# Softmax division of a windowed attention with channels on partitions: reciprocals spread on GpSimd and mapped by one matrix product

## What is computed

```python
x = x + attention(layernorm(x))         # softmax(q k^T / sqrt(8)) v, window 64, then @ Wo.T
x = x + experts(layernorm(x))           # sigmoid gate, 4 of 16 experts, silu(g) * u, plus a shared expert
# in attention:
p = jax.nn.softmax(scores, axis=-1)
out = jnp.einsum('bhnqk,bhnkd->bhnqd', p, v2)
out = out.transpose(0, 2, 1, 3).reshape(B, T, C)
return out @ Wo.T
```

## Time and profile before

| | |
|---|---|
| median of 3 runs | 708.99 us (707.56 to 709.00) |
| profiled execution | 710.96 us, its span 709.2 us |
| busy: PE, PEld, DVE, ACT, POOL | 93%, 74%, 83%, 75%, 67% |
| one slot of the loop | 40.1 us |

### The profile page before, as it was taken

The page is one execution under the profiler, slowest core; times in us unless marked ns, Lnnn a source line. Parts: engine busy times, 40 slices in busy tenths (PEclk is TensorE's granted clock), DMA queues, the critical chain, the costliest instruction groups (busy, mean ns, idle before and its releaser), DMA issues.

```text
span 709.2 us, 20018 instructions
## 1 busy us (share of the span) xinstructions
PE 662.5 (93%) x6488; PEld 521.9 (74%) x6488; DVE 590.6 (83%) x1708; ACT 530.9 (75%) x1635; POOL 478.5 (67%) x599
## 2 busy tenths in 40 slices
PE   3988889999999999999999999999999999989996
PEld 2767657777787877778787877778787877767775
DVE  2777797989989898988989898998989898888663
ACT  3775869787887879787887879787887879763432
POOL 3503157878788787877778687877878686776523
PEclk9998899999999999999999999999999999999999
DMA  6000022040414123040413113040313213041321
GB/s 174 20 13 31 1 73 96 17 141 28 130 50 120 59 74 105 19 131 30 122 58 116 63 63 117 12 137 30 120 59 105 74 56 110 6 134 35 117 76 46
DMA packets 50245, 52.60 MB, mean 74 GB/s; under 512 B 5664, under 2 KB 31904, under 8 KB 50080
## 3 DMA queue, kind: packets, MB, share of 16 engines
q1 hardware_dynamic: 50208, 52.14, 23.7%
HBM read 43.20 MB, written 4.72 MB: 68 GB/s over the span
## 4 chain that ended last, share of the span: by engine, by line
PE 30%; ACT 28%; DVE 19%; issue 12%; POOL 8%; DMA 1%; DVEq 1%; POOLq 0%; ACTq 0%; SPq 0%
ACT probs L603 12%; DVE neg_max L778 6%; PE PS L1057 5%; PE PS L903 4%; ACT q_by_head L554 4%; PE PS L865 4%; PE PS L867 4%; PE PS L866 4%; ACT v_bd L554 3%; ACT th L570 3%; DVE tu L767 3%; DVE probsT L738 3%; POOL hh L482 2%; POOL X L539 2%; POOL X L533 2%
## 5 line engine op out<-in xcount | busy, mean ns | idle before, releaser
L603 ACT ACTIVATE probs<-PS,neg_max 128x96 f32<-128x96 f32 (+1 forms) x1024 | 247.8, 351 | 75.7 <-DVE neg_max L778 75.7
L477 POOL TENSOR_TENSOR gate<-gate,spread 128x512 f32<-128x512 f32 x124 | 158.7, 1280 | 105.5 <-ACT gate L554 53.1
L482 POOL TENSOR_TENSOR hh<-gate,tu 128x512 f32<-128x512 f32 x108 | 139.3, 1290 | 14.7 <-DVE tu L767 7.3
L1057 PE MATMUL PS<-wd,hh 128*128 128x128 f32 x1024 | 137.5, 277 | 7.7 <-DVE OUT L793 2.9
L1057 PEld LDWEIGHTS PS<-wd,hh 128*128 128x128 f32 x1024 | 126.8, 192 | 20.7 <-DVE OUT L793 9.8
L778 DVE TENSOR_REDUCE neg_max<-PS 128x4 f32<-128x384 f32 (+1 forms) x256 | 122.1, 516 | 13.4 <-PE PS L903 11.7
L767 DVE SCALAR_TENSOR_TENSOR tu<-th,PS 128x512 f32<-128x512 f32 x128 | 87.5, 684 | 51.3 <-ACT th L570 39.5
L865 PE MATMUL PS<-x_hi,w_hi 128*128 128x512 f32 x288 | 125.0, 434 | 0.0
L570 ACT ACTIVATE th<-PS 128x512 f32<-128x512 f32 x128 | 80.5, 629 | 50.9 <-PE PS L867 49.3
L738 DVE STREAM_TRANSPOSE probsT<-probs 128x768 f32<-128x768 f32 (+1 forms) x128 | 114.4, 894 | 0.0
L867 PE MATMUL PS<-x_lo,w_hi 128*128 128x512 f32 x288 | 114.2, 397 | 0.0
(11 more groups left out here) (108 smaller groups left out, 986.9 us busy)
## 6 DMA issues: line engine op xcount, KB each, us to landing
spread<-weights_by_expert SPq DMA_DIRECT2D x248, 128.0 KB, 3.0
X<-x SPq DMA_DIRECT2D x32, 256.0 KB, 3.4
OUT<-H SPq DMA_DIRECT2D x16, 256.0 KB, 3.0
out<-OUT SPq DMA_DIRECT2D x16, 256.0 KB, 3.0
ffn_stage<-w_gu SPq DMA_DIRECT2D x1, 1152.0 KB, 7.0
wd<-w_down SPq DMA_DIRECT2D x1, 512.0 KB, 6.8
weights_by_expert<-cT SPq DMA_DIRECT2D x16, 32.0 KB, 1.6
probsT<-w_att SPq DMA_DIRECT2D x1, 192.0 KB, 3.1
```

Source lines behind the costliest of these rows:

```text
L477: tt(gate2[:, :], gate[:, k % 2, :], spread[:, k % SP_BUFS, :], ALU.mult).then_inc(s_g2, 1)
L482: tt(hh[:, k % 2, :], gate2[:, :], tu[:, k % 2, :], ALU.mult).then_inc(s_h, 1)
L603: ins = nc.scalar.activation(probs[:, u % PROB_BUFS, tt, 2 * rows + e, j0:KW], PS[:, rows, n * KW + j0:n * KW + KW], ACT.Exp, bias=neg_max ...
L1057: ins = mm(PS[:, 7, r], hh[:, k % 2, r], wd[:, k, :], start=(k == 0 and n == 0), stop=(k == NP - 1), skip_group_check=True)
```

## The change

The output stays with channels on partitions, and the reciprocals are brought there instead.

- DVE takes the reciprocal of `sums` in SBUF ahead of its 32x32 turn, in steps 5 and 0, with a wait for its own result between the two.
- POOL spreads `sums_t` into `by_block`: 128 x (8 blocks x 32 queries), masked so that each partition holds its values only in the columns of its own block (EXPAND, stages 14 and 17, steps 6 and 1, ahead of `gate2` of the step).
- PE makes one product, `to_channel` (128x128) with `by_block` (256 columns), into the shared bank; this takes the place of two transposes and four small products. DVE multiplies it with `o_f` straight into `oT`.
- ON is gone: two transposes on PE and one copy on ACT for each half group. The shared banks have 14 uses a slot where they had 16.
- The values product of the next half group waits for that DVE multiplication instead of the copy to `o_f`.
- Two masks and `to_channel` are made once at the start (two DVE reductions, four POOL products).
- The extra products L938 also run in steps 0 to 3 of slot 3 (`warming`).

The pieces of the diff stand in this order: the table of stages, POOL, ACT, DVE (two pieces), PE (four pieces).

```diff
-OT, ON, OW = 14, 15, 16
+EXPAND = (14, 17)
+OT, OW = 14, 16
...
+def warming(slot, s):
+    return filling(slot) or slot.fixed and slot.n == 3 and s < FF % STEPS
...
+                    for b, stage in enumerate(EXPAND):
+                        g, _ = at(sl, s, stage)
+                        if g:
+                            if not (g.fixed and g.n == 0):
+                                taken(pool, slot_before(sl), (OT + 4 * b) % STEPS, POST)
+                            pool.wait_ge(s_sum_t, g.n * GB + b + 1)
+                            whole = [P, NQ, Q]
+                            tt(by_block[:, b, :, :], sums_t[:, b, :].unsqueeze(1).broadcast_to(whole),
+                               block_of[:, :].unsqueeze(2).broadcast_to(whole), ALU.mult).then_inc(s_exp, 1)
...
-                    g, b = at(sl, s, ON, 4, GB)
-                    if g:
-                        side, bank = filled(act, sl, s, POST)
-                        copy(oT[:, :], bank[:, 0:T]).then_inc(s_taken[side], 1)
...
                             if u % 4 == 3:
                                 dve.wait_ge(s_sum, g.n * NU + u + 1)
+                                link(sl, v_.reciprocal(sums[:, b, :], sums[:, b, :]))
                                 v_.transpose(sums_t[:, b, :], sums[:, b, :]).then_inc(s_sum_t, 1)
...
-                        link(sl, v_.reciprocal(o_rs[:, :, :], bank[:, T:T + Q].rearrange("p (a v) -> p a v", v=4)))
-                        v_.tensor_tensor(o_n[:, :, :].rearrange("p n (a v d) -> p (n a) v d", v=4, d=D),
-                                         bank[:, 0:T].rearrange("p (a v d) -> p a v d", v=4, d=D),
-                                         o_rs[:, :, :].unsqueeze(3).broadcast_to([P, 8, 4, D]),
-                                         ALU.mult).then_inc(s_taken[side], 1)
+                        dve.wait_ge(s_o, g.n * GB + b + 1)
+                        v_.tensor_tensor(oT[:, :], o_f[:, :], bank[:, 0:T], ALU.mult).then_inc(s_taken[side], 1)
...
-                    if filling(sl) and at(sl, s, SC, 1, NU)[0]:
+                    if warming(sl, s) and at(sl, s, SC, 1, NU)[0]:
...
-                            pe.wait_ge(s_o, g.n * GB + b)
+                            taken(pe, slot_before(sl) if b else sl, (OT if b else OT + 4) % STEPS, POST)
...
-                        pe.wait_ge(s_o, g.n * GB + b + 1)
-                        for half in range(2):
-                            nc.tensor.transpose(bank[:, P * half:P * half + P], o_f[:, P * half:P * half + P], ident)
-                        pe.wait_ge(s_sum_t, g.n * GB + b + 1)
-                        for c in range(4):
-                            ins = mm(PS[32 * c:32 * c + 32, RING[side], T:T + Q], sums_t[:, b, :], sums_of[:, c, :, :, :],
-                                     start=True, stop=True)
-                        ins.then_inc(s_filled[side], 1)
-                    g, b = at(sl, s, ON, 4, GB)
-                    if g:
-                        side, bank = free(POST)
-                        taken(pe, sl, (s - 1) % STEPS, POST)
-                        for half in range(2):
-                            ins = nc.tensor.transpose(bank[:, P * half:P * half + P], o_n[:, half, :], ident)
-                        ins.then_inc(s_filled[side], 1)
+                        pe.wait_ge(s_exp, g.n * GB + b + 1)
+                        mm(bank[:, 0:T], to_channel[:, :], by_block[:, b, :, :].rearrange("p t q -> p (t q)"),
+                           start=True, stop=True).then_inc(s_filled[side], 1)
```

More of the change, by code:

```diff
@@ L69 @@
     (EARLY, (VP, LG)), (LATE, (XT, QP, KP, XT2, XT2 + 4, SH)),
-    (POST, (OT, OT + 4, ON, ON + 4, OW, OW + 4, SH)), (WEIGHTS, (CT,)))
+    (POST, (OT, OT + 4, OW, OW + 4, SH)), (WEIGHTS, (CT,)))
     for stage in stages])
@@ L220, in preln_block_kernel @@
         o_f = sb("o_f", [P, T])
-        o_rs = sb("o_rs", [P, 8, 4])
-        o_n = sb("o_n", [P, 2, P])
+        lane_of = sb("lane_of", [P, 4])
+        block_of = sb("block_of", [P, NQ])
+        to_channel = sb("to_channel", [P, P])
+        by_block = sb("by_block", [P, GB, NQ, Q])
         oT = sb("oT", [P, T])
@@ L275, in preln_block_kernel @@
         grouprow = const("grouprow")
-        sums_of = ident.rearrange("p (v h c a) -> p c h a v", v=4, h=2, c=4)
         def by_lane(n):
@@ L327, in preln_block_kernel @@
         s_sum_t = sem("sums_turned")
+        s_lane = sem("lane_masks_ready")
+        s_chan = sem("channel_map_ready")
+        s_exp = sem("reciprocals_by_block")
         s_o_ps = sem("o_in_psum")
@@ L463, in slot @@
                            ALU.subtract).then_inc(s_cst, 1)
+                    for b, stage in enumerate(EXPAND):
[7 more added lines that the diff above has]
+                               block_of[:, :].unsqueeze(2).broadcast_to(whole), ALU.mult).then_inc(s_exp, 1)
                     if sl.fixed and sl.n == 0 and s == LN1 + 1:
                         pool.wait_ge(s_w, 16 * LOADS)
+                        pool.wait_ge(s_lane, 1)
+                        for a in range(4):
+                            shape = [P, 4, D]
+                            ins = tt(to_channel[:, 32 * a:32 * a + 32].rearrange("p (v d) -> p v d", d=D),
+                                     lane_of[:, a:a + 1].unsqueeze(2).broadcast_to(shape),
+                                     grouprow.unsqueeze(2).broadcast_to(shape), ALU.mult)
+                        ins.then_inc(s_chan, 1)
                         nc.gpsimd.tensor_scalar(queryrow[:, :], headrow, Q_SCALE, 0.0, ALU.mult,
@@ L727, in slot @@
                         v_.tensor_copy(ident4[:, :], const("ident4"))
+                        v_.tensor_reduce(block_of[:, :], ident.rearrange("p (v t a) -> p t v a", t=NQ, a=HG),
+                                         mybir.AxisListType.XY, ALU.add)
+                        v_.tensor_reduce(lane_of[:, :], ident.rearrange("p (x a) -> p a x", a=HG),
+                                         AX_X, ALU.add).then_inc(s_lane, 1)
                         dve.wait_ge(s_cst, 1)
@@ L995, in slot @@
                         side, bank = free(POST)
-                        pe.wait_ge(s_o, g.n * GB + b + 1)
-                        for half in range(2):
-                            nc.tensor.transpose(bank[:, P * half:P * half + P], o_f[:, P * half:P * half + P], ident)
-                        pe.wait_ge(s_sum_t, g.n * GB + b + 1)
-                        for c in range(4):
-                            ins = mm(PS[32 * c:32 * c + 32, RING[side], T:T + Q], sums_t[:, b, :], sums_of[:, c, :, :, :],
-                                     start=True, stop=True)
-                        ins.then_inc(s_filled[side], 1)
-                    g, b = at(sl, s, ON, 4, GB)
-                    if g:
-                        side, bank = free(POST)
-                        taken(pe, sl, (s - 1) % STEPS, POST)
-                        for half in range(2):
-                            ins = nc.tensor.transpose(bank[:, P * half:P * half + P], o_n[:, half, :], ident)
-                        ins.then_inc(s_filled[side], 1)
+                        if g.fixed and g.n == 0:
+                            pe.wait_ge(s_chan, 1)
+                        pe.wait_ge(s_exp, g.n * GB + b + 1)
+                        mm(bank[:, 0:T], to_channel[:, :], by_block[:, b, :, :].rearrange("p t q -> p (t q)"),
+                           start=True, stop=True).then_inc(s_filled[side], 1)
                     g, b = at(sl, s, OW, 4, GB)
@@ L1013, in slot @@
                         side, bank = free(POST)
-                        taken(pe, slot_before(sl) if s == 0 else sl, (s - 1) % STEPS, POST)
+                        taken(pe, sl if b else slot_before(sl), (OT + 4 * b) % STEPS, POST)
                         if g.fixed and g.n == 0 and b == 0:
```

## The result

The changed kernel takes 754.36 us (median of 4 runs, 753.58 to 757.25), the one before 709.0 us in the same session (4 runs, 707.56 to 710.1). The ratio is 1.064 with a 95% interval of 1.0609 to 1.0672. I had forecast 709.5 us and a range up to 713.2: the kernel became slower by 45 us, and my slower case ended at +4.

The account below looks back on a forecast made before the run. PE, ACT and DVE were taken to bound the kernel together, PE without slack. Loop +0.4, slots 1 to 3 -0.7, slots 15 to 20 +0.8 gave +0.5 us: 709.5 us against the median of 708.99; range 705.0 to 713.2 us.

Parts of the forecast that it names:

- my slower case: Rival 3: each loop slot +0.3 us, in all +3.9 us and 713.4 us; chance 0.27.
- the loop with slot 3 and 15 has about 13 of them: Steady slots: +0.03 us each, about 13 slots, counted as +0.4 us in all.
- rival 3: Step 6: spreading ends late, at 390.8, so PE waits; +0.3 us a slot, +3.9 in all, 713.4 us; chance 0.27.
- The product: PE's new float32 product of 256 columns: 0.53 us, in place of OT's 0.59.
- The spreading: POOL, ahead of `gate2`: takes 0.61 us inside a 0.73 us idle gap, costing nothing on POOL.
- The wait at OT in step 6: PE, reaching OT at 390.08, waits for POOL's spreading until 390.6, idle about 0.5 us.
- The reciprocal on DVE: Ahead of `sums_t`: 0.28 us with its wait, making `tu` in step 5 0.1 us late.
- One slot: Net effect on a steady loop slot: +0.03 us; a slot of 40.0 to 40.2 us.
- rival 2: PE's saved 0.68 us a slot comes out in full: 8.8 us less, 700.7 us; chance 0.08.
- Slots 1 to 3: Start: shorter OT, reciprocals and ON off the chain, against +0.56 for the new reciprocal; together -0.7 us.
- Slots 15 to 20: End: PE waits for the spreading in slot 16, +2.1; ON -1.0, OT -0.3; together +0.8 us.
- rival 1: Slot 3: extra products L938 keep PE at full clock at 80 us; -1.6 us, 707.9 us; chance 0.23.

Follow-up runs that it names:

- the head at slot 0: Changed kernel with the start of TensorE's loop put at slot 0 of a 16-KB, 256-instruction code block: 707.74 us, ratio 0.9985.
- the head at 160 or 200: Changed kernel with the start of TensorE's loop put at instruction slot 160 or 200 of its 256-instruction code block: 708.68 us and 707.12 us.
- the product alone: Changed kernel without the extra products L938 in slot 3, start of TensorE's loop at slot 0 of a code block: 710.8 us, ratio 1.0013.
- the placed runs: Here the changed kernel with the start of TensorE's loop set to slot 0, 160 or 200 of its code block: 707.74, 708.68 and 707.12 us.
- the early spreading: Changed kernel, loop start at slot 0 of a code block, first half's spreading moved on GpSimd from step 6 to step 5, ahead of the norm: 707.06 us.
- the fillers alone: Kernel before plus only the 24 extra products L938 in slot 3, start of TensorE's loop at slot 0 of a code block: 706.76 us, ratio 0.9968.
- the old products with fillers: Kernel before plus only the 24 extra products L938 in slot 3, TensorE's loop start not placed, 48 instructions later: 744.05 us.
- The hint: Changed kernel with a hint to TensorE's queue, at the top of each loop pass, that its last branch will be taken: 711.69 us, ratio 1.0016.
- the head at 232: Changed kernel with the start of TensorE's loop put at slot 232 of its 256-instruction code block: 747.4 us.

## Why the prediction was wrong

**The step that failed** is the one from a slot to the loop, "the loop with slot 3 and 15 has about 13 of them". I took each pass as the sum of its slots and gave the branch back no term. It had one: 43.4 us in five passes. The trace of the kernel before had the facts for a doubt, q8 with 20 packets, so a program that is much longer than a pass, and PE's branch of 0.2 us, which is cheap only while the code is there. None of my four rivals was a price for where code lies. That the sign was among my cases, with a chance of 0.27, is luck: rival 3 named another mechanism, a late spreading, and the traces refute it as the cause.

**With that term taken out** by the head at slot 0, the forecast can be read step by step against 707.74 us (ratio 0.9985, interval over 1.0):

- *The product.* Forecast 0.53 us from start to next start; measured 628.38 - 627.87 = 0.51 (slot 16, above). Right.
- *The spreading.* Forecast 0.61; measured 0.61. It lies in the gap ahead of `gate`, as said.
- *The wait at OT in step 6.* Forecast about 0.5 us in each slot. Measured in a steady slot of that run, 0.17 (timeline, rows of DVE, GpSimd and PE):

```profile
385.87 0.35 DVE L781 RECIPROCAL sums<-sums 128x32 f32<-128x32 f32 x1
...
386.26 0.21 DVE L782 STREAM_TRANSPOSE sums_t<-sums 128x32 f32<-128x32 f32 x1
...
386.55 0.61 POOL L483 TENSOR_TENSOR by_block<-sums_t,block_of 128x256 f32<-128x256 f32 x1
...
387.22 0.70 PE L1025 MATMUL PS<-by_block,to_channel 128*128 128x256 f32 x2 [0.17 <-POOL by_block L483]
```

  The mechanism was right, the size was not. From the end of the sums the spreading takes to 387.16 - 385.87 = 1.29 us, where I had 390.5 - 388.99 = 1.5; and PE comes to the product 387.05 - 385.87 = 1.18 us behind them, where I had 390.08 - 388.99 = 1.09.
- *The reciprocal on DVE.* Forecast 0.28 with its wait; measured 386.26 - 385.87 = 0.39 to the start of the transpose behind it. Under-sized.
- *One slot.* Forecast +0.03 us; measured 40.03 against 40.07 (582.34 - 262.07 = 320.27 us in 8 slots with the head at 0, 585.69 - 265.13 = 320.56 before), so -0.04; with the head at 160 or 200 it is 40.00. The saved PE time did not come out (rival 2 had 39.4): PE is busy 38.62 us in a slot against 39.09, and idle for X, `fa`, `OUT` and the spreading in the rest. Right in kind.
- *Slots 1 to 3.* Forecast -0.7 us. The first `OUT` sum starts at 142.6 us with the product alone, against 143.95 to 144.9 in three runs with the old products; with the fillers the two kinds can't be told apart (140.8 to 142.3 in the placed runs against 141.1). The sign fits, the size is not resolved.
- *Slots 15 to 20.* Forecast a wait of 2.1 us in slot 16; measured 2.05 with the head at 0. (With the head at 160 and 200 it was 0.46 and 0.42, since there the lower clock had made PE late already.) The sum was +0.8, and that was too small: the stretch between the `OUT` sums of slots 16 and 17 is 33.8 to 36.6 us in the runs without a stall (six, the early spreading left out), and 32.2 to 33.6 with the old products (three), so some +2 to +3. The gain of ON and OT did not come out there. A term that I did not have is the clock: in four of the six it was 0.50 for 3.4 us of slot 16 (stretches of 35.1 to 36.6), in the other two and with the old products it stayed at 1.00 (33.8 and 34.5).
- *The clock in slot 3.* This was rival 1 with 0.23: -1.6 us, 707.9. It is what happened. The clock is at full speed from 75 to 85 us in the changed kernel too, and the fillers alone are worth 0.32%, 2.3 us (0.8 to 3.8 by the interval), against the 1.6 that I gave them.

So without the stall, rival 1 with 707.9 us would have been met by 707.74. That it fits so closely is partly luck: the end costs more than the +0.8 that I had, and the fillers and slots 1 to 3 seem to give more. A gain of the product's change on its own can't be seen: the fillers alone gave 0.9968, fillers and product together 0.9985, the product alone 1.0013. These intervals overlap or touch, so the order of the three is likely, not shown.

## What to carry to other kernels

A hardware loop whose body fills most of an engine's code store has a hidden term: when a change moves or resizes code ahead of the loop or in it, read the engine's own branch and the packets of the instruction queue before any engine's busy time. Give such a loop a fixed place (or a hint on its back edge) before comparing versions of it; otherwise one compares places. And fillers that keep TensorE's clock up are instructions too.

## What the runs showed of the hardware that I had not expected

- The price of a miss is far more than one fetch. In the changed kernel as written, with the head at about 252, it is 7.8 to 9.5 us a pass: 4.65 us without a product in the first pass and 5.1 to 6.75 in the later ones, in which two packets come one after the other, and then 6.8 to 10.2 us at half the clock. With the head further from the end it is 3 to 5.8 us where PE stands 2.4 to 2.9 us, and 5.5 to 8.6 where it stands 3.7 to 3.9 (the old products with fillers).
- After one miss every block of the pass is fetched again: 64 packets in place of 19 are 45, or 9 in each of five passes, although by theory A only the head's block was missing when the branch was taken. Each fetched block taking the place of the next one needed would explain it; no run shows that directly.
- The hint did not make the fetch earlier, it made it unnecessary: 19 packets in place of 64.
- Where the head lies near the end of its block, a trace with a miss tells its place: 24 instructions up to the second stall with the head at 232, 4 in the changed kernel.
- Sixteen empty instructions ahead of the loop moved nothing; 16 real ones took 45 us off.

What stays open: the exact edge (between 200 and about 204 for one body, between 96 and 160 for the other, so that "7 blocks of 256" is the rule that fits and is not proved). If the changed body has 1589 to 1592 slots, as 200 and 204 would have it, it is some 10 longer than the count without the waits, 1580, and I can't say by which instructions. Why the branch takes 5.1 us with the old products and fillers and 4.1 to 4.3 in the other misses is open too.
